# Eight exponentials, one extraction round and three shortened VectorE pieces in a four-layer graph network

## The reference

```python
h = jnp.maximum(_layernorm(x, axis=-1), 0.0);  x = x + _L0_gnn_ref(h, adj, ...)   # and so for L1, L2, L3
# L0: normalised aggregation: elu(einsum(adj, (h @ W) * norm) * norm + b), norm = (sum|adj| + eps)^-0.5
# L1: hyperbolic attention: att = sigmoid(left_i + right_j) * adj; u = logmap(h_i, h_j) for every pair of nodes
#     logmap needs atanh(|(-h_i) (+) h_j|) for 256x256 pairs; support = einsum(att, u); expmap(h, support)
# L2: message passing: sum_j adj_ij * gelu(layernorm(m_j + m_i + b1)); update = layernorm([h, agg] @ W2 + b2)
# L3: four steps of tanh([A' src, self, A'' dst] @ wu + bu), A' and A'' = adj with rows or columns of length one
```

## Time and profile before

| what | value |
|---|---|
| median of 3 runs | 3895.19 us |
| profiled execution, its own time | 3894.31 us |
| span of the profile, mean granted TensorE clock | 3892.5 us, 0.908 |
| busy: TensorE, VectorE, ScalarE, GpSimd | 3206.7, 3274.6, 2620.0, 1822.8 us |

### The profile page before, as it was taken

One profiled execution on the slowest core, in us unless ns is written; L12 is line 12 of the kernel. 1 busy time (PEld: TensorE's weight loads), 2 busy tenths in 40 slices (PEclk: granted clock), 3 DMA queues, 4 the chain that ended last, 5 costly groups with the idle time before them and its releaser, 6 DMA issues.

```text
span 3892.5 us, 89706 instructions
## 1 busy us (share of the span) xinstructions
PE 3206.7 (82%) x24327; PEld 2715.2 (70%) x24328; DVE 3274.6 (84%) x12083; ACT 2620.0 (67%) x6627; POOL 1822.8 (47%) x1288
## 2 busy tenths in 40 slices
PE   3484788898888889888888988888898888888898
PEld 2273667677676777767677776767777676786777
DVE  4889988989898898988889898988989888897930
ACT  2484775849667585866759586675858668594843
POOL 1172653719255272834628272552727346282720
PEclk7596889999898999989999998989999899999999
DMA  3010102011020200202021020202002020110200
GB/s 85 30 49 30 52 4 75 21 43 64 15 77 6 74 28 31 71 12 75 16 64 33 31 66 14 77 12 68 29 31 71 9 77 17 47 39 9 65 1 22
DMA packets 142473, 159.52 MB, mean 41 GB/s; under 512 B 12720, under 2 KB 100400, under 8 KB 142128
## 3 DMA queue, kind: packets, MB, share of 16 engines
q1 hardware_dynamic: 142128, 155.57, 13.3%
HBM read 142.94 MB, written 12.58 MB: 40 GB/s over the span
## 4 chain that ended last, share of the span: by engine, by line
PE 24%; issue 23%; POOL 23%; ACT 13%; DVE 13%; DVEq 1%; POOLq 1%; ACTq 1%; DMA 0%; SPq 0%
POOL v_z L570 16%; PE n_bank_c L1619 7%; POOL v_prstd L577 5%; PE n_bank_d L1636 4%; PE n_bank_d L1637 4%; PE n_bank_d L1633 3%; ACT v_diag L777 2%; ACT v_rows L815 2%; PE n_bank_b L1694 2%; PE n_bank_c L1615 1%; PE n_bank_a L1504 1%; DVE v_normed L1182 1%; ACT v_pair L880 1%; ACT v_junk L679 1%; DVE v_tangent L1332 1%
## 5 line engine op out<-in xcount | busy, mean ns | idle before, releaser
L570 POOL TENSOR_TENSOR v_z<-v_z,all_bc_L_gnn_be 128x512 f32<-128x512 f32 x620 | 787.5, 1271 | 84.1 <-DVE v_z L1136 74.6
L777 ACT ACTIVATE v_diag<-all_ident,v_value 128x128 f32<-128x128 f32 x2480 | 754.0, 386 | 0.3
L1535 PE MATMUL n_bank_d<-v_diag,v_msg 128*128 128x128 f32 x4960 | 630.9, 281 | 46.0 <-ACT v_msg L772 23.3
L577 POOL TENSOR_TENSOR v_prstd<-v_pvar,all_neg_half 128x8 f32<-128x8 f32 x310 | 511.5, 1650 | 268.0 <-DVE v_pvar L1129 238.1
L1535 PEld LDWEIGHTS n_bank_d<-v_diag,v_msg 128*128 128x128 f32 x4960 | 587.1, 194 | 54.2 <-issue 27.9
L1619 PE MATMUL n_bank_c<-all_l_wsd,v_fT 128*128 128x256 f32 x1792 | 455.8, 397 | 0.0
L1526 PE MATMUL n_bank_b<-v_parts,v_onehot 128*128 128x128 f16 x4960 | 343.7, 227 | 124.7 <-ACT n_bank_b L726 124.6
L721 ACT ACTIVATE v_fT<-n_bank_d,all_l_c 128x256 f32<-128x256 f32 x256 | 119.7, 473 | 460.8 <-PE n_bank_d L1637 460.6
L1526 PEld LDWEIGHTS n_bank_b<-v_parts,v_onehot 128*128 128x128 f16 x4960 | 296.8, 101 | 173.9 <-ACT n_bank_b L726 162.5
L1526 PE MATMUL n_bank_c<-v_parts,v_onehot 128*128 128x128 f16 x4960 | 340.5, 225 | 83.8 <-ACT n_bank_c L726 83.6
L1619 PEld LDWEIGHTS n_bank_c<-all_l_wsd,v_fT 128*128 128x128 f32 x1792 | 359.1, 200 | 69.1 <-issue 0.5
(11 more groups left out here) (278 smaller groups left out, 6672.0 us busy)
## 6 DMA issues: line engine op xcount, KB each, us to landing
v_spread<-slot_rows SPq DMA_DIRECT2D x310, 256.0 KB, 3.2
v_adj_l<-in_adj SPq DMA_DIRECT2D x128, 256.0 KB, 4.2
v_adj_x<-in_adj SPq DMA_DIRECT2D x64, 256.0 KB, 3.8
v_ring<-in_x SPq DMA_DIRECT2D x16, 512.0 KB, 5.8
out_x<-v_xout SPq DMA_DIRECT2D x64, 128.0 KB, 1.9
slot_rows<-v_indexT SPq DMA_DIRECT2D x16, 256.0 KB, 2.0
w_wu<-in_L_gnn_wu SPq DMA_DIRECT2D x4, 192.0 KB, 2.5
all_W<-in_L_gnn_W SPq DMA_DIRECT2D x2, 128.0 KB, 4.3
```

Source lines behind the costliest of these rows:

```text
L570: nc.gpsimd.tensor_tensor(z[par][:, units], z[par][:, units], wide(bc["L2_gnn_be1"])[:, units], ALU.add).then_inc(sem["z_ready"], 1)
L577: nc.gpsimd.tensor_tensor(prstd[:, par], pvar[:], minus_half, ALU.pow).then_inc(sem["prstd_ready"], 1)
L777: ins = nc.scalar.activation(diag[par][:, u], ident[:], ACT.Copy, scale=value[:, u, bass.ds(slot, 1)])
L1535: ins = nc.tensor.matmul(ps_agg[:, u // NB, (u % NB) * P:(u % NB + 1) * P], msg[par][:, u], diag[par][:, u], start=False, stop=False, skip ...
```

## The change

It makes five edits; the first three are on VectorE.

1. Layer norm statistics: one BN_STATS over two interleaved tiles in place of two, read directly, without BN_AGGR; the variance is scaled by 1/D in the instruction that adds epsilon.
2. Layer 0: `layer0_normed` goes, and with it eight tile products; `layer0_scaled` first multiplies the two scales (`both`), normalises with the product, and takes the maximum with zero over two tiles at a time.
3. `coefficients`: the product of `total` and `gate` moves to GpSimd (four products behind `rstd3`, semaphore `weight_ready`), and VectorE does one operation for each graph in place of two.
4. `ratios` moves from behind the first round of the extraction to the place before its last.
5. On ScalarE the eight exponentials move from before `keep_sd(2, 0)` to behind `keep_sd(2, 3)`.

```diff
@@ gpsimd, mix
+                if l1:
+                    for b in range(GB):
+                        pool.wait_ge(sem["coef_ready"], done + (b + 1))
+                        nc.gpsimd.tensor_tensor(gate[:, b], total[:, b], gate[:, b], ALU.mult).then_inc(sem["weight_ready"], 1)
@@ scalar, mix
-                if l1:
-                    for b in range(GB):
-                        act.wait_ge(sem["diff_ready"], a * GB + (b + 1))
-                        nc.scalar.activation(pair[:, b, 0], pair[:, b, 0], ACT.Exp, scale=0.5).then_inc(sem["s_ready"], 1)
-                        nc.scalar.activation(total[:, b], total[:, b], ACT.Exp, scale=-0.5).then_inc(sem["coef_ready"], 1)
                 if l3:
                     keep_sd(t, 2, 0)
                     keep_sd(t, 2, 1)
...
                 if l3:
                     keep_sd(t, 2, 2)
                     keep_sd(t, 2, 3)
+                if l1:
+                    for b in range(GB):
+                        act.wait_ge(sem["diff_ready"], a * GB + (b + 1))
+                        nc.scalar.activation(pair[:, b, 0], pair[:, b, 0], ACT.Exp, scale=0.5).then_inc(sem["s_ready"], 1)
+                        nc.scalar.activation(total[:, b], total[:, b], ACT.Exp, scale=-0.5).then_inc(sem["coef_ready"], 1)
                 if l1:
                     act.preload_act_table_set(LN_EXP_TABLES)
@@ vector
-            def layernorm_sums(xg, stat, mean_var):
-                for u in range(UNITS):
-                    v.bn_stats(stat[:, u], xg[:, u])
-                dve.drain()
-                for u in range(UNITS):
-                    ins = v.bn_aggr(mean_var[:, u], stat[:, u])
+            def layernorm_sums(xg, stat):
+                for q in range(UNITS // 2):
+                    ins = v.bn_stats(stat[:, 2 * q:2 * q + 2].rearrange("p u c -> p (u c)"),
+                                     xg[:, 2 * q:2 * q + 2].rearrange("p u d -> p d u"))
                 return ins
+
+            def spread_of(stat, var_):
+                return v.tensor_scalar(var_[:], stat[:, :, 2], 1.0 / D, LN_EPS, ALU.mult, ALU.add)
...
-            def layer0_normed(z_):
+            def layer0_scaled(z_):
                 dve.wait_ge(sem["rstd0_ready"], z_ + 1)
+                dve.wait_ge(sem["norm_ready"], z_ + 1)
+                v.tensor_tensor(both[:], rstd[:], norm[:], ALU.mult)
+                dve.drain()
                 xg = nodes(z_)
                 for u in range(UNITS):
-                    v.tensor_scalar(normed[:, u], xg[:, u], mv0[:, u, 0:1], rstd[:, u:u + 1], ALU.subtract, ALU.mult)
+                    v.tensor_scalar(normed[:, u], xg[:, u], mv0[:, u, 1:2], both[:, u:u + 1], ALU.subtract, ALU.mult)
                 dve.drain()
...
-                    for u in range(b * NB, (b + 1) * NB):
-                        ins = v.tensor_scalar(hn[:, u], normed[:, u], 0.0, norm[:, u:u + 1], ALU.max, ALU.mult)
-                    ins.then_inc(sem["hn_ready"], 1)
+                    v.tensor_scalar(hn[:, of(b)], normed[:, of(b)], 0.0, None, ALU.max).then_inc(sem["hn_ready"], 1)
...
                 eight(0, True)
-                between()
                 with dve.Fori(1, full) as r:
                     eight(r, True)
+                between()
                 eight(full, False)
...
-                        dve.wait_ge(sem["coef_ready"], a * GB + (b + 1))
-                        v.scalar_tensor_tensor(total[:, b], pair[:, b, 0], 0.5, total[:, b], ALU.mult, ALU.mult)
-                    dve.drain()
-                    for b in range(GB):
-                        dve.wait_ge(sem["gated"], a * GB + (b + 1))
-                        v.tensor_tensor(pair[:, b, 0], total[:, b], gate[:, b], ALU.mult).then_inc(sem["c_ready"], 1)
+                        dve.wait_ge(sem["weight_ready"], a * GB + (b + 1))
+                        v.scalar_tensor_tensor(pair[:, b, 0], pair[:, b, 0], 0.5, gate[:, b], ALU.mult, ALU.mult)\
+                            .then_inc(sem["c_ready"], 1)
```

More of the change, by code:

```diff
@@ L309, in network @@
         norm = plan.sb("norm", [P, UNITS])
-        stats = plan.sb("stats", [P, UNITS, 6])
-        mv = plan.sb("mv", [P, UNITS, 2])
-        mv0 = plan.sb("mv0", [P, UNITS, 2])
+        both = plan.sb("both", [P, UNITS])
+        mv = plan.sb("mv", [P, UNITS, 3])
+        mv0 = plan.sb("mv0", [P, UNITS, 3])
         var = plan.sb("var", [P, UNITS])
@@ L331, in network @@
         negatives = plan.view("negatives", [P, UNITS], at)
-        nstats = plan.sb("nstats", [P, UNITS, 6])
-        nmv = plan.sb("nmv", [P, UNITS, 2])
+        nmv = plan.sb("nmv", [P, UNITS, 3])
         nvar = plan.sb("nvar", [P, UNITS])
@@ L341, in network @@
         inv = plan.sb("inv", [P, GB, 2, NB])
-        mv3 = plan.sb("mv3", [P, UNITS, 2])
+        mv3 = plan.sb("mv3", [P, UNITS, 3])
         var3 = plan.sb("var3", [P, UNITS])
@@ L995, in layer0_stats @@
                 dve.sem_inc(keep["held"], 1)
-                layernorm_sums(nodes(z_), stats, mv0)
+                layernorm_sums(nodes(z_), mv0)
                 dve.drain()
-                v.tensor_scalar(var[:], mv0[:, :, 1], LN_EPS, None, ALU.add).then_inc(sem["var0_ready"], 1)
+                spread_of(mv0, var).then_inc(sem["var0_ready"], 1)
             def layer0_eps(z_):
@@ L1038, in layer0_moved @@
                 dve.sem_inc(keep["held"], 1)
-                for u in range(UNITS):
-                    v.bn_stats(stats[:, u], xg[:, u])
+                layernorm_sums(xg, mv)
                 dve.drain()
             def layer0_variance(z_):
-                for u in range(UNITS):
-                    v.bn_aggr(mv[:, u], stats[:, u])
-                dve.drain()
-                v.tensor_scalar(var[:], mv[:, :, 1], LN_EPS, None, ALU.add).then_inc(sem["var1_ready"], 1)
+                spread_of(mv, var).then_inc(sem["var1_ready"], 1)
             def needed_slots(a):
@@ L1089, in take_slots @@
                 eight(0, True)
-                between()
                 with dve.Fori(1, full) as r:
                     eight(r, True)
+                between()
                 eight(full, False)
             def node_stats(a):
-                layernorm_sums(nodes(a), nstats, nmv)
+                layernorm_sums(nodes(a), nmv)
                 dve.drain()
-                v.tensor_scalar(nvar[:], nmv[:, :, 1], LN_EPS, None, ALU.add).then_inc(sem["nvar_ready"], 1)
+                spread_of(nmv, nvar).then_inc(sem["nvar_ready"], 1)
             def normalise_nodes(a):
@@ L1230, in update_stats @@
                     dve.drain()
-                    layernorm_sums(upd, nstats, nmv)
+                    layernorm_sums(upd, nmv)
                     dve.drain()
-                    v.tensor_scalar(nvar[:], nmv[:, :, 1], LN_EPS, None, ALU.add).then_inc(sem["upd_var_ready"], 1)
+                    spread_of(nmv, nvar).then_inc(sem["upd_var_ready"], 1)
                 def update_normed():
@@ L1247, in update_x @@
                     dve.sem_inc(keep["held"], 1)
-                    layernorm_sums(xg, nstats, mv3).then_inc(sem["mv3_ready"], 1)
+                    layernorm_sums(xg, mv3).then_inc(sem["mv3_ready"], 1)
                 def last_normed(units):
@@ L1254, in last_normed @@
                     for i in units:
-                        v.tensor_scalar(flat[:, i], xg[:, i], mv3[:, i, 0:1], rstd3[:, i:i + 1], ALU.subtract, ALU.mult)
+                        v.tensor_scalar(flat[:, i], xg[:, i], mv3[:, i, 1:2], rstd3[:, i:i + 1], ALU.subtract, ALU.mult)
                 def last_features():
@@ L1401, in mix @@
                     update_normed()
-                if l0:
-                    layer0_normed(z_)
                 if l3:
@@ L1463, in mix @@
                     pick(first_ahead + 1, 1)
-            for piece in (layer0_stats, layer0_eps, layer0_normed, layer0_scaled, layer0_z, layer0_moved, layer0_variance):
+            for piece in (layer0_stats, layer0_eps, layer0_scaled, layer0_z, layer0_moved, layer0_variance):
                 piece(0)
```

13 lines of the change are left out of this document (5 added, 8 removed).

## The result

The changed kernel takes **3920.42 us** (median of 7 runs, 3910.81 to 3927.19) against 3890.19 us for the kernel before in the same measurement (median of 7): ratio **1.0072**, 95% interval 1.0054 to 1.0091, 30 us slower. The forecast was 3928 us.

A forecast was written before the change was run, and what follows sets the result against it. The prediction took TensorE's list, held up by ScalarE, to bound a full mix from the gates to layer 3's end; 13 full mixes at +3.84 gave +50, the others -16, so +34 on 3894.3: 3928 us, range 3898 to 3958.

The forecast's parts named there:

- The exponentials, +4.16: ScalarE, ahead of the second logarithms' table load: moved exponentials lengthen TensorE's wait at `l3_f(2, 2)` by 4.16 us per full mix.
- The clock behind the gap, +2.0: TensorE behind the wait at `l3_f(2, 2)`: slower granted clock costs 2.0 us per full mix, bounds 1.65 and 4.4.
- The differences, 0: VectorE's differences, moved ahead of the extraction's last round: ready earlier or in time, nobody waited for them, 0 us per full mix.
- The scaling and GpSimd's products, 0: Two terms, layer 0's scaling covered by a wait for TensorE and four products moved to GpSimd: 0 us each per full mix.
- The rule that the prediction cites: Two-SBUF-input VectorE and SBUF-reading GpSimd instructions exclude each other; products would hold VectorE up for as much as 5.9 us.
- Statistics, early, -0.92: `layer0_stats` early in a full mix: four statistics release ScalarE 0.92 us earlier, all passed on to the gates; bounds 0.7 and 1.0.
- The end, -1.4: End of a full mix: VectorE's tail 1.5 us shorter, ScalarE's copies limiting the gain to 1.4 us, bounds 0.6 and 1.5.
- a rival, at 0.7 us and chance 0.05: Change does little: larger early and late gains, clock up at the end too, 0.7 us a mix, 3895 to 3905; chance 0.05.
- The other mixes, -16: Mixes other than the 13 full ones, and the prologue: g = -1 and 0 save 6 and 7 us, together -16.

The follow-up runs named there:

- exps_only: The kernel before with only the eight exponentials of each mix moved behind the third terms' copies, differences left in place: 3955.61 us, ratio 1.0165.
- filled_ten: The changed kernel with 10 further products nobody reads, per full mix, in TensorE's wait ahead of the third scores: 3893.57 us, ratio 1.0000.
- half_moved: The changed kernel with the exponentials of the first two groups back in the old place, the last two groups' left behind the copies: 3871.74 us, ratio 0.9934.
- exps_back: The changed kernel with the eight exponentials of each mix back in their old place, all else of the change kept: 3834.38 us, ratio 0.9846.
- both_back: The changed kernel with exponentials and differences both back in their old places, leaving VectorE's three savings: 3835.99 us, ratio 0.9856.
- stats_only: The kernel before with one edit alone, the statistics over interleaved pairs without aggregation: 3835.18 us, ratio 0.9843.

## Why the prediction was right, and where it was not

- **The exponentials, +4.16: right.** The wait grew from 0.73 to 4.89 us. B grew by 4.2 (before to after) and 3.9 (before to exps_only; 4.2 in eleven of its mixes, while in the other two the clock stayed up at the turned adjacency). Put back, they gave 86 us, more than the kernel had lost.
- **The clock behind the gap, +2.0: right, 1.7 measured** (C, 15.0 against 13.3; filled_ten takes it away in every mix). The bounds were 1.65 and 4.4; half_moved shows that 3.1 occurs too.
- **The differences, 0: right.** exps_back and both_back differ by 1.6 us in 3835.
- **The scaling and GpSimd's products, 0: right.** stats_only and both_back differ by 0.8 us, and their ratios by less than their intervals. The products do hold VectorE up, three pieces of `clip` in 3.92 us in place of 1.1, but no logarithm came later for it: the eight behind the table load run without a gap. The rule that the prediction cites is one for two inputs, and `clip` has one. The Trainium skill (SBUF — State Buffer, Who interferes with whom) lists `tensor_scalar` among the operations that can take the port pair shared with GpSimd; the trace agrees, with the 3.92 us in place of 1.1.
- **Statistics, early, -0.92: 0.7 measured** in A between before and after, 0.5 between before and stats_only. The clamp itself came as much sooner as forecast: 1.58 us behind the start of the statistics in g = 3 where it was 2.52. Not all of that reached the logarithms; which step kept the rest was not followed.
- **The end, -1.4: the step that was wrong, 2.7 measured.** The forecast counted the shorter chain of VectorE, bounded by 1.5, and put nothing for TensorE's clock there. That part is about 1.0 (E of 12.2 with the statistics, 13.2 without them where the clock stays up). The other 1.6 is the clock, which fell behind the 1.7-us wait in every full mix before and no longer does. The forecast had this only as a rival, at 0.7 us and chance 0.05, though the slow products could have been read from the timeline of the kernel before, where four take 1.11 us beside 0.66 and eight take 2.63 beside 1.89:

```profile
1100.38 0.66 PE L1839 MATMUL n_bank_b<-all_ident,v_normed 128*128 128x128 f32 x4 [1.73 <-DVE v_normed L1104]
1101.40 1.11 PE L1839 MATMUL n_bank_b<-all_ident,v_normed 128*128 128x128 f32 x4 [0.37 <-DVE v_normed L1104]
...
1103.16 2.63 PE L1849 MATMUL n_bank_b<-all_W,v_hT 128*128 128x256 f32 x8
1105.63 1.89 PE L1849 MATMUL n_bank_c<-all_W,v_hT 128*128 128x256 f32 x8
```

- **The other mixes, -16: too large.** g = -1 and 0 gave 4.4 and 3.5 us (6 and 7 forecast): in g = 0 the four `clamp_pair` wait 7.5 us for TensorE where they waited 3.0 before, so that probably most of what the shorter scaling saves is lost there; no run tried it. In g = 14 the wait for v_fT grew from 3.52 to 6.7 us and the mix by 1.8 (forecast -1). The exponentials did not replace the wait there; 3.2 of their 4.16 us came on top of it.

A full mix costs 2.5 us where 3.84 were forecast, 17 us less in 13 mixes. The other mixes and what lies around them gave 7 us in place of 16, and the slots came out 7 us longer in this trace. So the sum, +33 us of span against +34, is closer than its terms, and that is luck: an end that gained more was made up for by other mixes that gained less and by slots that differ from trace to trace. The medians differ by 30 us.

## What to carry to other kernels

Work moved on an engine that is not the bottleneck is priced by where it stands in that engine's list. Here it was free ahead of a gap, and in a gapless piece that ends in something TensorE waits for it cost its whole length and a fall of the clock behind it. Read the products behind TensorE's waits, not the waits alone: behind waits of 1.7 us and more a fall cost mostly 1.6 us or more here, and a shorter chain that ended the wait gained it back. Where such a wait cannot go, filling it with idle products that end before it does gave 17 to 27 us each time; filling past its end cost more than the clock.

## What the hardware showed unexpectedly

The length of a wait does not decide whether TensorE's clock falls. Behind the 0.7 us ahead of the third scores it never fell in the traces of before and exps_back; behind 4.9 us in each of 13 mixes. Behind 2.81 us it fell in six of 13 in one kernel, behind 1.7 us at the end of the mix in every full mix of the kernel before and in five of 13 of exps_only. Behind 2.6 us at the turned adjacency it fell in all 13 in the kernel before, in eleven in exps_back and in eight in filled_ten. Nor does the length decide the price: 1.6 us at the end and at the turned adjacency, 1.7 behind 4.9 us (2.0 in the one mix of 13, g = 6, where TensorE worked 4.0 us at half clock in place of 3.4), up to 3.1 behind 2.81. What decides it is how long TensorE works at half clock: half of that time was lost each time it was compared (1.7 of 3.4, 2.0 of 4.0, 3.1 of 6.1). The Trainium skill (TensorE: Matmul & The Clock Gate, The HAM clock gate) says that the number of slow products at the start of one and the same kernel varies between runs; here it varies between mixes of one execution, at equal instructions and equal waits at that place. What puts a mix on one side or the other was not tried, and stays open.
